# Decays, keys and mixes of an RWKV time mixing in PSUM, with a new order of its work and values of one group made beside it

## The reference

```python
xn = _ln(x, ln1_w, ln1_b);  sx = _token_shift(xn, state[:, i1])
xxx = jnp.tanh((xn + sx * maa_x) @ maa_w1).reshape(b, l, 5, 1, 32)
xxx = jnp.matmul(xxx, maa_w2).reshape(b, l, 5, E)
x5 = xn[:, :, None] + sx[:, :, None] * (maa_stack + xxx)          # five mixes
w = jnp.exp(-jnp.exp(time_decay + jnp.tanh(x5[:, :, 1] @ decay_w1) @ decay_w2))
r, k, v = x5[:, :, 3] @ Wr.T, x5[:, :, 0] @ Wk.T, x5[:, :, 2] @ Wv.T
g = jax.nn.silu(x5[:, :, 4] @ Wg.T)
def step(s, rkvw):                                                # scan over 112 positions
    a = k_t[:, :, :, None] * v_t[:, :, None, :]
    out = jnp.einsum('bhk,bhkd->bhd', r_t, u * a + s)
    return (a + w_t[:, :, :, None] * s, out)
att = (a4 - m) * rsqrt(var + EPS) * gn_w + gn_b                   # per head of 16
x = x + att * g @ Wo.T
xn2 = _ln(x, ...);  x = x + sigmoid(xr @ ffn_Wr.T) * (square(relu(xk @ ffn_Wk.T)) @ ffn_Wv.T)
# first cross-attention, per group of 4 heads (G = 4 groups) and batch row:
vh = (kv_in @ wv + bv);  kh = (kv_in @ wk + bk);  ctx = softmax(q k) v;  x = res + ctx @ wo + bo
```

## Time and profile before

| | us |
|---|---|
| median of three runs | 3475.76 |
| the profiled execution | 3479.91 |
| its span | 3478.6 |
| TensorE busy | 3122.2 (90%) |
| VectorE busy | 1403.1 (40%) |
| ScalarE busy | 1171.9 (34%) |
| GpSimd busy | 1111.1 (32%) |
| mean granted TensorE clock | 0.949 |

### The profile page before, as it was taken

The page is one execution under the profiler, slowest core; times in us unless marked ns, Lnnn a source line. Parts: engine busy times, 40 slices in busy tenths (PEclk is TensorE's granted clock), DMA queues, the critical chain, the costliest instruction groups (busy, mean ns, idle before and its releaser), DMA issues.

```text
span 3478.6 us, 44113 instructions
## 1 busy us (share of the span) xinstructions
PE 3122.2 (90%) x16568; PEld 2580.5 (74%) x16568; DVE 1403.1 (40%) x2992; ACT 1171.9 (34%) x2637; POOL 1111.1 (32%) x986
## 2 busy tenths in 40 slices
PE   4787988879599999999999999999899998888988
PEld 1454555557498989898988888988778777667876
DVE  4499328931333333344333333323411255552133
ACT  3322322332343333344223222223333344444321
POOL 5555235532312222223112121221344133335410
PEclk8799988989799999999999999999999999989999
DMA  6566346724233333333112121221011110101122
GB/s 222 169 213 187 104 139 201 221 90 154 93 127 132 119 131 119 131 126 135 61 66 96 66 84 71 79 96 54 31 61 49 65 41 23 41 33 64 49 90 86
DMA packets 142064, 358.30 MB, mean 103 GB/s; under 512 B 13008, under 2 KB 82128, under 8 KB 133024
## 3 DMA queue, kind: packets, MB, share of 16 engines
q1 hardware_dynamic: 141376, 354.81, 30.5%
q10 hardware_dynamic: 480, 0.69, 0.1%
HBM read 314.81 MB, written 40.63 MB: 102 GB/s over the span
## 4 chain that ended last, share of the span: by engine, by line
PE 66%; DVE 8%; POOL 7%; DMA 7%; ACT 7%; issue 5%; SPq 1%; POOLq 0%; ACTq 0%; DVEq 0%
PE bank L176 19%; PE bank L178 18%; PE bank L177 18%; PE bank L1728 5%; POOL W_lo L216 3%; DMA W_lo<-ctx_split 3%; ACT W_hi L207 2%; PE bank L1713 1%; DMA W_raw<-in_weights 1%; ACT prob L2406 1%; PE bank L620 1%; DVE max L1921 1%; DVE K_lo L258 1%; ACT prob L1810 1%; ACT K_hi L249 1%
## 5 line engine op out<-in xcount | busy, mean ns | idle before, releaser
L2002 POOL TENSOR_SCALAR prob<-prob,inverse 112x376 f32<-112x376 f32 x256 | 144.3, 584 | 1121.8 <-DVE inverse L1927 1121.8
L216 POOL TENSOR_TENSOR W_lo<-W_raw,W_hi 128x1024 fp32r<-128x1024 f32 x138 | 331.1, 2421 | 187.6 <-ACT W_hi L207 184.9
L176 PE MATMUL bank<-ctx_hi,W_hi 128*128 128x376 f32 x1024 | 355.7, 347 | 25.1 <-DVE K_lo L258 19.6
L258 DVE SCALAR_TENSOR_TENSOR K_lo<-bank,vectors,K_hi 128x375 fp32r<-128x375 f32 (+1 forms) x288 | 173.8, 607 | 452.6 <-ACT K_hi L249 452.6
L176 PE MATMUL bank<-W_hi 128*128 128x512 f32 (+2 forms) x608 | 281.1, 462 | 77.5 <-DMA W_lo<-ctx_split 51.7
L177 PE MATMUL bank<-ctx_lo,W_hi 128*128 128x376 f32 x1024 | 344.8, 337 | 0.0
L178 PE MATMUL bank<-ctx_hi,W_lo 128*128 128x376 f32 x1024 | 344.4, 336 | 0.0
L176 PE MATMUL bank<-act_hi,W_hi 128*128 128x448 f32 x800 | 312.4, 390 | 30.8 <-POOLq L333 10.9
L177 PE MATMUL bank<-act_lo,W_hi 128*128 128x448 f32 x800 | 299.5, 374 | 0.0
L178 PE MATMUL bank<-act_hi,W_lo 128*128 128x448 f32 x800 | 299.0, 374 | 0.0
L249 ACT ACTIVATE K_hi<-bank,vectors 128x375 fp32r<-128x375 f32 (+1 forms) x288 | 163.5, 577 | 296.3 <-PE bank L178 296.3
(11 more groups left out here) (247 smaller groups left out, 6679.3 us busy)
## 6 DMA issues: line engine op xcount, KB each, us to landing
W_raw<-in_weights SPq DMA_DIRECT2D x69, 1024.0 KB, 4.9
ctx_hi<-ctx_split SPq DMA_DIRECT2D x64, 752.0 KB, 5.5
ctx_lo<-ctx_split SPq DMA_DIRECT2D x64, 752.0 KB, 7.0
v_spread<-v_rows SPq DMA_DIRECT2D x128, 224.0 KB
W_hi<-ctx_split SPq DMA_DIRECT2D x128, 188.0 KB, 3.3
W_lo<-ctx_split SPq DMA_DIRECT2D x128, 188.0 KB, 4.5
values<-value_rows SPq DMA_DIRECT2D x64, 256.0 KB
V<-values SPq DMA_DIRECT2D x32, 512.0 KB, 3.9
```

The lines of the kernel that those rows point to most:

```text
L176: nc.tensor.matmul(dst, left[0], right[0], start=first, stop=False)
L216: pool.tensor_tensor(k.Wl[:, slot, cs, :], k.Wraw[:, cs, :], k.Wh[:, slot, cs, :].bitcast(F32), ALU.subtract).then_inc(*k.w_low.now((n, i)))
L258: dve.scalar_tensor_tensor(out=low, in0=src, scalar=bias, in1=high.bitcast(F32), op0=ALU.add, op1=ALU.subtract).then_inc(*k.banks.draining ...
L2002: pool.tensor_scalar(k.Pm[:, h, :], k.Pm[:, h, :], k.rsum[:, h:h + 1], 1.0, ALU.mult, ALU.mult).then_inc(*k.prob_done.now((n, h)))
```

## The change

1. The decays of a chunk o are copied into bank 2 and its keys into bank 5, 16 steps at a time, and scan and outer product read them there. Mixes are made in place in their bank, and their low part by VectorE instead of GpSimd.
2. The order ahead of a recurrence is mixes 2, v, mixes 0, mixes 1, decays, mixes 3, then chunk 0 of k and r alone. The other chunks of k and r are made in steps 0 to 11, mixes 4 in steps 10 to 16, and all four gates inside the recurrence (GATE_AT). Of the splits of context, 8 halves stay ahead of recurrence 0 and 8 go ahead of recurrence 1.
3. The variance of a head is summed with positions in lanes (112 x 32), its reciprocal taken there, and the root, spread over the head's 16 rows by ScalarE, is turned back by four transposes (pe_spread_root).
4. The end of half 0 (last chunk's centre, variance, root, gate and the product with Wo) is issued among the mixes of half 1. The end of half 1 makes the first three chunks of its output while that last chunk is under way.
5. MADE = 1: V of group 0 alone is made beside the recurrences, one quantum at each of steps 13 to 60, and none elsewhere. Units 8 to 31 make their V in the attention, as units 32 to 63 do.

The diff, cut:

```diff
...
+MADE = 1
+ORDER = (["v", "k", "v1_0", "r", "g", "o", "v", "r", "k"] + [f"v1_{g}" for g in range(1, MADE)] + ["g", "o", "fr", "fk", "fv"]
+         + [f"{w}1_{g}" for g in range(G) for w in ("qko" if g < MADE else "qkvo")] + UNIQUE[UNIQUE.index("q2_0"):])
 NSLOT = 4
-W_TIME = [{w: ORDER.index(w, at) for w in "krvgo"} for at in (0, 7)]
-W_VALUES = [ORDER.index(f"v1_{g}") for g in range(G)]
+SECOND = ORDER.index("v", 1)
...
+    if m in (8, 9):
+        sp.wait_ge(*k.gated_low[0, C - 1])
...
+PER_HALF = len(FILLS) // 2
+
+
+POINTS = [(half, n) for half in range(2) for n in range(64)]
+FILL_FROM, FILL_TO = 13, 61
+QUANTA_AT = [MADE if FILL_FROM <= n < FILL_TO else 0 for half, n in POINTS]
+assert sum(QUANTA_AT) == NQ * len(FILLS)
...
+MIXES = (2, 0, 1, 3)
+MIX_SLOT = {2: 0, 0: 0, 1: 1, 3: 1, 4: 0}
+
+LATE_KR = [("k", 1), ("r", 1), ("k", 2), ("k", 3), ("r", 2), ("r", 3)]
+MIX4_AT = 10
+GATE_AT = {17: (0, 0), 19: (0, 1), 21: (0, 2), 23: (0, 3), 33: (1, 0), 35: (1, 1), 37: (1, 2), 39: (1, 3),
+           49: (2, 0), 50: (2, 1), 51: (2, 2), 52: (2, 3), 54: (3, 0), 55: (3, 1), 56: (3, 2), 57: (3, 3)}
+GATE_OUT_AT = {24: 0, 40: 1, 53: 2, 58: 3}
+TURN_AT = (24, 32, 40, 48)
+
+DECAY_BANK, KEY_BANK = 2, 5
...
+        keys = [("mix", half, 2, c) for c in range(C)] + [("v", half, o) for o in range(C)]
+        keys += [("mix", half, 0, c) for c in range(C)] + [("mix", half, 1, c) for c in range(C)] + [("dec1", half)]
+        keys += [("mix", half, 3, c) for c in range(C)] + [("dec2", half, c) for c in range(C)]
+        keys += [("k", half, 0), ("r", half, 0)]
+        if half:
+            tail(k, 0)
+        u.rotate(keys, [0, 1, 6])
+        u.rotate([(name, half, o) for name, o in LATE_KR], [0, 1])
+        plan_values(k, half)
...
+def pe_late_kr(k, half, n):
+    if n < 2 * len(LATE_KR):
+        name, o = LATE_KR[n // 2]
+        for c in (0, 1) if n % 2 == 0 else (2, 3):
+            pe_project(k, half, name, o, c)
...
-    pe_heads(k, ("var", half, o), k.mx[:, 0])
+
+    pe, key = k.nc.tensor, ("var", half, o)
+    pe.wait_ge(*k.squared[half, o])
+    pe.wait_ge(*k.banks.free(key))
+    bank = k.banks.tile(key)
+    for b in range(HB):
+        m = pe.matmul(bank[0:T, 8 * b:8 * b + 8], k.mx[:, 0, b, :], k.heads[:, 0:P:S0], start=True, stop=True)
+    m.then_inc(*k.banks.filling(key))
+
+def pe_spread_root(k, half, o):
+
+    pe, key = k.nc.tensor, ("rstd", half, o)
+    pe.wait_ge(*k.rooted[half, o])
+    pe.wait_ge(*k.banks.free(key))
+    bank = k.banks.tile(key)
+    for b in range(HB):
+        m = pe.transpose(bank[:, columns(b)], k.head_root[:, b * P:(b + 1) * P], k.ident[0:T, 0:T])
+    m.then_inc(*k.banks.filling(key))
...
+            pe_mix(k, half, 2, c)
+            if half and c == 2:
+                pe_centre(k, 0, C - 1)
+        for o in range(C):
+            for c in range(C):
+                pe_project(k, half, "v", o, c)
+            if half and o == 0:
+                pe_variance(k, 0, C - 1)
+            if half and o == 1:
+                pe_spread_root(k, 0, C - 1)
         for c in range(C):
             pe_mix(k, half, 0, c)
-            if half:
-                pe_fill(k, ("pre", 1, 1 + c))
-        if half == 0:
-            pe.wait_ge(k.decay_loaded, 32)
-            pe.wait_ge(k.rec_loaded, 48)
-        key = ("dec1", half)
-        pe.wait_ge(*k.banks.free(key))
-        dst = k.banks.tile(key)[0:64, 0:HALF]
+        if half:
+            for i in range(HB):
+                pe_out_chunks(k, 0, i, range(C))
         for c in range(C):
-            pe.wait_ge(*k.x5_low[half, 1, c])
-            xh, xl = x_in_slot(k, 0, c)
-            pe.matmul(dst, k.dec_w1[:, c, :], xh.bitcast(F32), start=c == 0, stop=False)
-            m = pe.matmul(dst, k.dec_w1[:, c, :], xl.bitcast(F32), start=False, stop=c == C - 1)
-        m.then_inc(*k.banks.filling(key))
+            pe_mix(k, half, 1, c)
+        pe_decay(k, half)
         for c in range(C):
             pe_mix(k, half, 3, c)
-            if half:
-                pe_fill(k, ("pre", 1, 5 + c))
-        pe.wait_ge(*k.banks.drained(("dec1", half)))
-        for c in range(C):
-            key = ("dec2", half, c)
-            pe.wait_ge(*k.banks.free(key))
-            pe.matmul(k.banks.tile(key)[:, 0:HALF], k.dec_w2[:, c * P:(c + 1) * P], k.thd[:], start=True,
-                      stop=True).then_inc(*k.banks.filling(key))
-        pe_project_rwkv(k, half, "k", 0, W_TIME[half]["k"])
-        if half:
-            pe_fill(k, ("pre", 1, 9))
-        for c in range(C):
-            pe_mix(k, half, 2, c)
-            if half:
-                pe_fill(k, ("pre", 1, 10 + c))
-        pe_project_rwkv(k, half, "r", 3, W_TIME[half]["r"])
-        pe_project_rwkv(k, half, "v", 2, W_TIME[half]["v"])
+        pe_decay_out(k, half)
+        if half == 0:
+            pe.wait_ge(k.rec_loaded, 48)
+        for name in "kr":
+            for c in range(C):
+                pe_project(k, half, name, 0, c)
...
+            pe_late_kr(k, half, n)
+            if MIX4_AT <= n < MIX4_AT + C:
+                pe_mix(k, half, 4, n - MIX4_AT)
+            if n in GATE_AT:
+                pe_project(k, half, "gate", *GATE_AT[n])
             if d == 3 and o:
                 pe_centre(k, half, o - 1)
-            pe_fill(k, ("rec", half, n))
+            pe_fill(k, half, n)
...
+    pe_out_chunks(k, 1, 0, range(C - 1))
+    pe_centre(k, 1, C - 1)
+    pe_out_chunks(k, 1, 1, range(C - 1))
+    pe_out_chunks(k, 1, 2, range(C - 1))
+    pe_variance(k, 1, C - 1)
+    pe_out_chunks(k, 1, 3, range(C - 1))
+    pe_spread_root(k, 1, C - 1)
+    for i in range(HB):
+        pe_out_chunks(k, 1, i, range(C - 1, C))
...
+def act_keys_to_bank(k, half, o):
+
+    act = k.nc.scalar
+    act.wait_ge(*k.banks.drained(("k", half, o)))
+    if o or half:
+        act.wait_ge(*k.outer_done[(half, S0 * o - 1) if o else (half - 1, 63)])
+    act.copy(k.bank[KEY_BANK][:, 0:HALF], flat(k.kT[:, o])).then_inc(*k.keys_banked.now((half, o)))
+
+def act_decay_to_bank(k, half, o):
+
+    act = k.nc.scalar
+    act.wait_ge(*k.decay_done[half, o])
+    if o or half:
+        act.wait_ge(*k.scan_done[(half, S0 * o - 1) if o else (half - 1, 63)])
+    act.copy(k.bank[DECAY_BANK][:, 0:HB * (T + 1)], flat(k.wT[:, o])).then_inc(*k.decay_banked.now((half, o)))
...
+    act.wait_ge(*k.head_var[half, o])
+    act.activation(k.head_root[:].rearrange("t (g d) -> t g d", d=S0), k.inv_var[:].broadcast_to([T, 8 * HB, S0]),
+                   ACT.Sqrt).then_inc(*k.rooted.now((half, o)))
...
+            if d == S0 - 1 and o < C - 1:
+                act_keys_to_bank(k, half, o + 1)
...
+            if n == 9:
+                act_split_weight(k, w["g"])
+            if n == 14:
                 act_split_weight(k, w["o"])
-            act_fill(k, ("rec", half, n))
-            if group_ends_at(("rec", half, n)) in (0, 1):
-                act_split_weight(k, W_VALUES[group_ends_at(("rec", half, n)) + 1])
-        if half:
-            act_fill(k, ("post", 1))
-        act_gate(k, half, C - 1)
-        act_square(k, half, C - 1)
-        act_root(k, half, C - 1)
-        act_gated(k, half, C - 1)
-        act_split_weight(k, W_TIME[1]["k"] if half == 0 else W_FFN["fr"])
+            if n == 59:
+                act_split_weight(k, W_TIME[1]["v"] if half == 0 else W_FFN["fr"])
...
+    dve, own, key = k.nc.vector, k.dve_own, ("mix", half, j, c)
+    bank = by_batch(k.banks.tile(key)[:, 0:HALF])
+    dve.wait_ge(*k.banks.filled(key))
+    own.step(dve.scalar_tensor_tensor(out=bank, in0=bank, scalar=V(k, f"maa_{j}", c), in1=k.sx[:, c], op0=ALU.add, op1=ALU.mult))
+    own.settle()
+    dve.tensor_tensor(bank, bank, k.xn[:, c, :, 1:T + 1], ALU.add).then_inc(*k.x5_done.now((half, j, c)))
+
+def dve_mix_low(k, half, j, c):
     dve, key = k.nc.vector, ("mix", half, j, c)
-    a, b = scratch(k, j, c)
-    dve.wait_ge(*k.banks.filled(key))
-    if half and j == 1 and c < 2:
-        dve.wait_ge(*k.y_done[0, 62 + c])
-    if j == 4 and c == 0:
-        dve.wait_ge(*k.banks.filled(("rank2", half)))
-    if j == 4 and c:
-        dve.wait_ge(*k.x5_done[half, 4, c - 1])
-    dve.scalar_tensor_tensor(out=a, in0=by_batch(k.banks.tile(key)[:, 0:HALF]), scalar=V(k, f"maa_{j}", c), in1=k.sx[:, c],
-                             op0=ALU.add, op1=ALU.mult).then_inc(*k.banks.draining(key))
-    dve.wait_ge(*k.banks.drained(key))
-    if before := scratch_before(half, j, c):
-        dve.wait_ge(*k.x5_low[before])
-    if half and j == 1 and c < 2:
-        dve.wait_ge(*placed(k, 0, 62 + c))
-    dve.tensor_tensor(b, a, k.xn[:, c, :, 1:T + 1], ALU.add).then_inc(*k.x5_done.now((half, j, c)))
+    xh, xl = x_in_slot(k, MIX_SLOT[j], c)
+    dve.wait_ge(*k.x5_high[half, j, c])
+    dve.tensor_tensor(xl, k.banks.tile(key)[:, 0:HALF], xh.bitcast(F32), ALU.subtract).then_inc(*k.banks.draining(key))
...
-        dve.wait_ge(*k.banks.drained(("k", half, o)))
-    dve.tensor_tensor(state_tile(k, n)[:, :, 1:T + 1], k.vb[:, n % 4], k.kT[:, o],
```

(30 more changed lines are left out.)

705 lines of the change are left out of this document (316 added, 389 removed).

## The result

The changed kernel takes 3370.65 us (median of four runs, 3365.9 to 3378.28), the kernel before 3476.52 us beside it: a ratio of 0.9692, 95% interval 0.9665 to 0.9719. It is 106 us faster. The profiled execution took 3365.9 us with a span of 3364.6, so it gained 114.0 us on the span of before.

The account below looks back on a forecast made before the run. VectorE, with TensorE close behind, bounds the recurrences; chains of waits the stretches in front; TensorE is busiest in feed-forward. +174 - 72 - 32 - 55 + 0 - 76 = -61 us gives 3419, against the median 3415; range 3350 to 3470.

Parts of the forecast that it names:

- The V term: Attention layer, units 8 to 31: making V in place there costs +173.9 us, nothing hidden; called the surest term.
- VectorE's sum: Each recurrence: 126 us against 178, with scans and outer products at their shortest time because one input is in a bank.
- Rival 2: Recurrences: banks bring nothing, scans and outer products keep 1.50 and 0.84 us; VectorE 171, 198 us a half, 3491; chance 0.05.
- Rival 3: Scans and outer products: a source in a bank has a fixed price of 79 ns, 20 us in all, 3435; chance 0.05.
- The recurrence's pace: Each recurrence: TensorE at 139 us, a little the longer engine, times 1.11 gives 154; with a new wait 160, together -72.
- The wait for weight o: Each recurrence, load at step 13 and split at step 14: a new wait of 6 us a half, from 0 to 10.
- Rival 4: Recurrences: spread values come late through four buffers, 2.9 us a step, 184 us a half, 3463; chance 0.08.
- Rival 5: Engines mesh better: 140 us a half in the recurrences, 20 less ahead of the second: 3355; chance 0.12.
- Rival 1: Recurrences: TensorE rests more and its clock falls; slower than before under a granted clock of 0.71 (199 us a half); chance 0.07.
- The stretch between the recurrences: Ahead of recurrence 1, a chain of waits: start at 445 instead of 500, -55 us, bounds -80 and -20.
- The first stretch: Ahead of recurrence 0, weights and context halves end last: start at 111 instead of 143, -32 us, bounds -45 and -10.
- Feed-forward: Feed-forward stage: 96 quanta leave, it ends at about 789 instead of 865, -76 us, bounds -60 and -88.

Follow-up runs that it names:

- experiment 1: Changed kernel, but the scan reads the decays from their SBUF tile again: 3405.6 us, ratio 0.9807.
- experiment 2: Changed kernel, but scans read decays from SBUF and outer products read keys from SBUF too, except in chunk 3: 3438.7 us, ratio 0.9903.
- experiment 3: Changed kernel, but each quantum of V makes only one matmul of three, without the low products: 3366.2 us, ratio 0.9695.
- experiment 7: Kernel before with the move of V alone (group 0 in the recurrences, groups 1 to 3 in the attention): 3485.1 us, ratio 1.0024.
- experiment 6: Changed kernel, but each quantum of V makes its three matmuls twice: 3410.6 us, ratio 0.9801.
- experiment 5: Changed kernel with a fifth buffer for spread values and only the first matmul of each quantum of V: 3352.6 us, ratio 0.9635.
- experiment 8: Changed kernel with all sixteen context halves ahead of recurrence 0 and none ahead of recurrence 1: 3392.4 us, ratio 0.9766.
- experiment 9: Changed kernel, but ScalarE splits the weight r after the four casts of mixes 0: 3366.0 us, ratio 0.9669.
- experiment 10: Changed kernel with r split later as in experiment 9, and the first two context halves of each stretch directly behind mixes 0: 3359.1 us, ratio 0.9654.
- experiment 4: Changed kernel with a fifth buffer for spread values, each load issued five steps ahead: 3367.1 us, ratio 0.9697.

## Why the prediction was right, and where it was off

**The V term** holds: +180.2 against +174, of which unit 7 to 31 is 686.7 us against the 682.0 that I took:

```profile
L1930 DVE TENSOR_REDUCE max<-bank x4: 539/540/540, 799.0 to 800.4; 112x1 f32<-112x376 f32 x4
...
L1930 DVE TENSOR_REDUCE max<-bank x4: 540/545/549, 1485.7 to 1487.1; 112x1 f32<-112x376 f32 x4
```

The 4.7 more lie at one border: unit 7 to 8, where made V gives way to V made in place, takes 41.2 us, the borders after it 36.9 and 36.6.

**VectorE's sum** was 126 and measured 126.1. The reading behind it, that an instruction with an input in a bank doesn't stretch, was shown by experiments 1 and 2, which give 68 of the 106 us back. Of the row that I took it from, L992, I wrote that all 32 lie beside GpSimd work; the trace has 19 of them so and 13 alone, both at 671 to 685 ns, so the reading stands. Rival 2 falls with the experiments: its sum for VectorE, 171, is near the 169 of experiment 2, but the recurrence is 176 us with it, not 198. Rival 3 falls too. The shortest scans are 1084 and 1083 ns from SBUF in experiment 2, 1084 and 1066 from the bank, and the outer products from SBUF (experiment 2) and from the bank (the changed kernel) have medians 1 ns apart:

```profile
L1039 DVE TENSOR_TENSOR state<-v_spread,kT x48: 591/611/2730, 104.7 to 513.0; 128x448 f32<-128x448 f32 x48
L1038 DVE TENSOR_TENSOR state<-v_spread,bank x64: 560/610/622, 104.9 to 485.4; 128x448 f32<-128x448 f32 x64
```

A fixed price of 79 ns for each is not there. The fixed price that the Trainium skill gives in "VectorE: DVE Perf Modes", the section on the TRN2 errata, doesn't show in these runs.

**The recurrence's pace** is the step that failed: TensorE at 139 us, and from it, by "a factor of 1.11", a stage of 154. TensorE measured 128.75 and 127.71, at a granted 0.92 and 0.93. My 125 us at full clock were too many by 6 to 7 (128.75 x 0.92 = 118, an estimate), and the clock didn't stay at 0.90. "TensorE becomes a little the longer of the two" holds by 2 to 3 us of busy time, but it doesn't bound: with 112 us in experiment 3 the stage stays at 143 to 144.

What is added to the longer engine is neither the factor nor an amount that stays. In the kernel before and in the changed one VectorE idles 20 us a half (199 less 178, 146 less 126), and 129 x 1.11 = 143 comes near as well; that both fit is luck, as the waits are other ones (their lines stand in the section on the result), and other runs have neither. VectorE idles 5.5 us where it is busy 180 and TensorE 130 (experiment 7), 7.5 at 169 and 137 (experiment 2), 10 at 150 and 132 (experiment 1), 20 at 126 and 129. In experiment 6 TensorE is the longer, 158 to 124, and idles 10. So the stage is near the longer engine's sum where the other is 30 us or more behind, and some 20 us over it where they are equal. At 18 us apart both occur: 10 in experiment 1, 20 in the kernel before. Late spreads come on top: with a fifth buffer and a shorter TensorE together 13 us are left (experiment 5), with the shorter TensorE alone 18 (experiment 3). This is a pattern over eight kernels; how the waits follow from one another step by step wasn't traced.

**The wait for weight o**, 6 us a half, didn't come: ScalarE waited 0 and 1.0 us for a weight in the recurrences. SP issued it at 133.3 (steps 12 to 13) and ScalarE split it at 139.2, as VectorE's own steps at that point, with the mixes 4, take 3.3 to 5.1 us each, so the load has the time it needs. I had given them the mean of a stage of 160 us, 2.5.

**Rival 4**, spreads that come late, was there in a small size: 14.8 and 10.5 us of waits, not 2.9 us in each step.

**Rival 5**, engines that mesh better, came nearest: its 140 us a half were 145 and 143, but its 20 us more ahead of the second recurrence were 5.

**Rival 1**, the clock, didn't come in the changed kernel. Its 0.71 was wrong besides: if 125 us of matmuls fill 199, the granted clock would be 125 / 199 = 0.63. Experiment 7 shows that its mechanism exists: with 48 quanta a half and VectorE still slow, TensorE is busy 130 of 186 us and is granted 0.82 and 0.79, against 0.90 and 0.91 before. It didn't cost there, as VectorE set the pace.

**The stretch between the recurrences** had the right size for a wrong reason. I forecast 342 to 445 instead of 500 and put it to the new order and to the values' way through memory. Experiment 7 takes V's 56 quanta out of it, with their context chunks and copies, and gets 54.5 of the 60.4 us. The row was there: TensorE is busy 140 of 158 us in that stretch of the earlier trace rows, and the sentence "no engine is near full" was wrong for it: VectorE's 178 of 199 in the recurrence is hardly a larger share. The rest of the change then gives 11.4 (104.3 to 92.9 in experiment 8) and the eight context halves take 5.5 of these back. Of the chain that I had called the bound, experiment 9 still takes 5.5 us.

**The first stretch** was right in size, and in cause in part. The forecast had the context halves in the chain that ends last, but named the values' way through memory first. With the new order and all sixteen halves the first scan comes at 136.1 (experiment 8), so the rest of the change gives 6.9 of the 36.2 us and the eight halves that left give 29.3. What ends last with eight stays open: experiments 9 and 10 move that stretch by no more than its scatter.

**Feed-forward**, -94.8 against -76. I set all 96 quanta into the 149 us up to the first addition; there the difference is 149.0 to 65.5, -83.5, within my bounds, and 10.5 more come behind it, where 11 of the quanta lay (by TensorE's records behind 865) and where I had put 0. Some 4 us of the rest belong to this one execution: the stretch from the last scan to unit 0 takes 170.8 in it, and 172 to 176 in the kernels of the twelve experiments, at a granted clock of 0.80 to 0.81 instead of 0.83 in those looked at.

Put together, by the ratios: V moved alone +8 us; banks for decays and keys -73; eight context halves moved -26; all else (order, roots with positions in lanes, low parts on VectorE, the end of half 0 among mixes 2) some -16. Taken from the intervals of the ratios, the second and third have some 14 to 16 us to either side and the last some 19, so by the times alone it isn't clear of zero; the 6.9 and 11.4 us of the two stretches in front speak for it. Its parts weren't tried one by one. What the banks are worth without the move of V wasn't tried, as the values hold three banks there. Experiment 6 comes near it: with TensorE at 158 and 159 us, about what the kernel before has (160 and 165), but with banks and the new order, the recurrences take 167 and 168 us, against 198 and 192. So about half of the gain there doesn't hang on the move, though this compares kernels that differ in more than the banks.

## What to carry to other kernels

Sum each engine by stage, and then look at how far the second one is behind. In these runs the longer engine idled 5.5 to 10 us of a recurrence where the other was 30 us or more behind, and some 20 where the two were equal; neither the old factor nor the old amount of idle time carries over by itself. Before a stretch is called a chain of waits, look for fillers in it: here fillers made up an engine that was 88% busy, and taking them out gave what the reordering was credited with. A filler in a gap is free only up to the next limit. V's low matmuls cost 1 us of both recurrences at one quantum a step, 8 once the fifth buffer had taken a part of the spreads' waits (experiments 3 to 5), and the second quantum a step two thirds of its time or more. A stage read from one trace needs the same stage of kernels that leave it alone beside it: here it scattered by 3 to 5 us.
